# Attention block on one core: one 512 KB transposing DMA for both halves of a tile's probabilities

## Chip, cores and metric

One core of one Trainium2 chip. The metric is the device time of one execution in microseconds, the median of three runs. TensorE ran at its upper clock level, 2.4 GHz, through the whole profiled execution (granted clock 1.000).

## What is computed

The reference is an attention block with group normalisation in float32 on `x` of 4 x 128 x 32 x 32, so 4 batches of 128 channels and N = 1024 positions:

```python
h = x.reshape(B, GROUPS, C // GROUPS, N)            # 32 groups of 4 channels
h = (h - mean) * rsqrt(var + 1e-6)                  # over a group's channels and positions
h = h.reshape(B, C, N) * gamma[None, :, None] + beta[None, :, None]
qkv = einsum('oc,bcn->bon', w_qkv, h) + b_qkv       # q, k, v: 128 channels each
attn = softmax(einsum('bqc,bkc->bqk', q, k) / sqrt(C), axis=-1)
out = einsum('bqk,bkc->bqc', attn, v)
out = einsum('oc,bcn->bon', w_proj, out.transpose(0, 2, 1)) + b_proj
return x + out.reshape(B, C, H, W)
```

## The kernel before

The products that carry the accuracy are done in halves: a float32 value is split into a float16 high half and a float16 low half (the value less the high half), and three products (high by high, high by low, low by high) stand for one. The weights are folded ahead: `a_mat` joins the query and key weights, so that one product of `z` (the normalised input) gives `t`, and `t` by `z` gives the scores; `w_mat` joins the value and projection weights, so that `v` already holds the projected values.

The work is cut into G = 32 tiles of 128 query rows: 4 batches (b) of 8 tiles (s). A tile `g` goes through these steps, each on its own engine, held together by semaphores that count:

1. `score_tile(g)` on TensorE (lines 617 to 619): six matmuls of 512 columns give the 128 x 1024 scores in one of two PSUM slots. It waits until the exponential of tile g-2 has read the slot, and for `t_lo` of its batch half.
2. `maxima(g)` on VectorE (L432, L435): the row maximum and the bias of the exponential.
3. `exponentials(g)` on ScalarE (L343) writes `probs`, a ring of RING = 4 tiles; `p_high(g)` on ScalarE (L350) rounds it to the high half, `p_hl[:, g % RING, 0]`. It waits until the transposition of the high half of tile g-4 has landed.
4. `p_low(g)` on GpSimd (L285) writes the low half, `p_hl[:, g % RING, 1]`. It waits for the high half, and for the landing of tile g-4's low half.
5. SP transposes each half, 128 x 1024 float16 or 256 KB, by a DMA into `ptT`, a ring of PT_RING = 6 tiles (L232 the high half when it is made, L235 the low half when it is made).
6. `values(g)` on TensorE (lines 632, 633, 637): 16 matmuls of the high half against `v_hi` and `v_lo`, then, behind the wait for the low half's landing, 8 of the low half against `v_hi`, all 128 x 128 x 128 into one PSUM area.
7. `scale_output(g)` (L447), a turn on TensorE (L643) and `add_input(g)` (L453) finish the tile; SP stores four tiles at a time (L225).

The order of work is written out by hand, and each engine runs its own program in order. TensorE's loop takes, in step g: `score_tile(g)`, the turn of tile g-5, `values(g - 4)` (LAG = 4), and in some steps the products for `v` and for the next batch's `t`. So a tile's transpositions have about four steps of TensorE to land, and value matmuls that wait hold back the next score tile behind them. SP's program in step g: a wait that TensorE is done with tile g-6 (a free place in `ptT`), the wait for the high half and its DMA, the wait for the low half and its DMA, and, in every fourth step from 8 on, a store of tiles g-8 to g-5. GpSimd also normalises the next batch between its low halves: for batch 1 in steps 1, 3 and 4, for the later ones spread over the steps (lines 291 to 311).

Of the kernel before, what the change touches and what calls it, by code (L numbers as in the profile page):

```python
# [12 lines left out]
P = 128  # L13
B = 4
N = 1024
# [3 lines left out]
TILES = N // P  # L19
# [3 lines left out]
RING = 4  # L23
PT_RING = 6
# [12 lines left out]
def attention_block(nc, x, gamma, beta, w_qkv, b_qkv, w_proj, b_proj, out):  # L37
# [4 lines left out]
    with ExitStack() as ctx:  # L42
        def sb(name, shape, dt=F32):
            return ctx.enter_context(nc.sbuf_tensor(name, shape, dt))
# [4 lines left out]
        def sem(name):  # L49
            return ctx.enter_context(nc.semaphore(name))  # L50
# [56 lines left out]
        v_hi = sb("v_hi", [P, B * N], F16)  # L107
# [7 lines left out]
        p_hl = sb("p_hl", [P, RING, 2, N], F16)  # L115
        ptT = sb("ptT", [P, PT_RING, 2, TILES, P], F16)
# [71 lines left out]
        exp_ready = sem("exp_ready")  # L188
        phi_ready = sem("phi_ready")
        plo_ready = sem("plo_ready")  # L190
        hi_transposed = [sem(f"hi_transposed{i}") for i in range(RING)]
        lo_transposed = [sem(f"lo_transposed{i}") for i in range(RING)]
        pv_ready = sem("pv_ready")
        rinv_ready = sem("rinv_ready")
        oT_ready = sem("oT_ready")
# [8 lines left out]
        def wait(eng, s, value):  # L204
            if value > 0:
                eng.wait_ge(s, value)
# [3 lines left out]
        @block.sync  # L210
        def _(sp):
            for half in range(2):
                cols = slice(half * HALF, (half + 1) * HALF)
                sp.dma_start(x_sb[:, cols], x_d[0, :, cols]).then_inc(x_first[half], 16)
            sp.dma_start(beta_c[:], col(beta)).then_inc(c_loaded, 16)
            sp.dma_start(bq_c[:], col(b_qkv[0:P])).then_inc(c_loaded, 16)
            sp.wait_ge(wqk_loaded, 16)
            sp.wait_ge(gcol_loaded, 16)
            for b in range(1, B):
                sp.dma_start(x_sb[:, b * N:(b + 1) * N], x_d[b]).then_inc(x_rest[b - 1], 16)  # L220

            def store(first, tiles):
                b, s = divmod(first, TILES)
                sp.wait_ge(out_ready, first + tiles)
                sp.dma_start(out_d[b, :, s * P:(s + tiles) * P],  # L225
                             out_sb[:, first * P:(first + tiles) * P]).then_inc(stored, 16)

            for g in range(G):

                wait(sp, pv_ready, g - PT_RING + 1)  # L230
                sp.wait_ge(phi_ready, g + 1)
                sp.dma_start(ptT[:, g % PT_RING, 0], p_hl[:, g % RING, 0], transpose=True  # L232
                             ).then_inc(hi_transposed[g % RING], 16)
                sp.wait_ge(plo_ready, g + 1)
                sp.dma_start(ptT[:, g % PT_RING, 1], p_hl[:, g % RING, 1], transpose=True  # L235
                             ).then_inc(lo_transposed[g % RING], 16)
                done = g - LAG - CT
                if done >= 0 and done % CT == 0:
                    store(done, CT)
            for first in range(G - 2 * CT, G - CT, CT):  # L240
                store(first, CT)
            store(G - CT, CT - 1)
            store(G - 1, 1)
            sp.wait_ge(stored, 16 * (G // CT + 1))

        @block.gpsimd
        def _(pool):
            nc.gpsimd.memset(zero32[:], 0.0).then_inc(zeroed, 1)
            pool.wait_ge(zeroed, 1)
            nc.gpsimd.affine_select(out=ident32[:], in_=zero32[:], compare_op=ALU.not_equal, fill=1.0, base=0,  # L250
                                    pattern=[[-1, P]], channel_multiplier=1).then_inc(consts, 1)
            pool.dma_start(bv_c[:], col(b_qkv[2 * P:3 * P])).then_inc(o_loaded, 16)
            pool.dma_start(bp_c[:], col(b_proj)).then_inc(o_loaded, 16)

            def power(b):
                pool.wait_ge(vareps_ready, b + 1)
                nc.gpsimd.tensor_tensor(rstd[:, b:b + 1], var_eps[:, b:b + 1], minus_half[:], ALU.pow  # L257
                                        ).then_inc(rstd_ready, 1)

            def normalise(b, half):  # L260
                pool.wait_ge(rstd_ready, b + 1)

                pool.wait_ge(zlo_ready, b * 2)
                cols = slice(half * HALF, (half + 1) * HALF)
                nc.gpsimd.tensor_scalar(z32[:, cols], x_sb[:, b * N + half * HALF:b * N + (half + 1) * HALF],
                                        neg_mean[:, b:b + 1], rstd[:, b:b + 1], ALU.add, ALU.mult
                                        ).then_inc(z_ready, 1)

            def z_high(b, half):
                cols = slice(half * HALF, (half + 1) * HALF)  # L270
                pool.wait_ge(z_ready, b * 2 + half + 1)
                nc.gpsimd.tensor_copy(z_hi[:, b * N + half * HALF:b * N + (half + 1) * HALF], z32[:, cols]
                                      ).then_inc(zhi_ready, 1)

            def z_low(b, half):
                to = slice(b * N + half * HALF, b * N + (half + 1) * HALF)
                pool.wait_ge(zhi_ready, b * 2 + half + 1)
                nc.gpsimd.tensor_tensor(z_lo[:, to], z32[:, half * HALF:(half + 1) * HALF], z_hi[:, to],
                                        ALU.subtract).then_inc(zlo_ready, 1)

            def p_low(g):
                pool.wait_ge(phi_ready, g + 1)

                wait(pool, lo_transposed[g % RING], 16 * (g // RING))
                nc.gpsimd.tensor_tensor(p_hl[:, g % RING, 1], probs[:, g % RING], p_hl[:, g % RING, 0],  # L285
                                        ALU.subtract).then_inc(plo_ready, 1)

            pool.wait_ge(const_dve, 2)
            power(0)

            for g in range(G):
                b, s = divmod(g, TILES)
                p_low(g)
                if g == 1:
                    power(1)
                    normalise(1, 0)
                    normalise(1, 1)
                if g in (3, 4):
                    z_low(1, g - 3)

                if s == 7 and b + 2 < B:
                    power(b + 2)
                    normalise(b + 2, 0)

                if b >= 1 and b + 1 < B:
                    if s == 0:
                        normalise(b + 1, 1)
                    if s in (1, 3):
                        z_high(b + 1, s // 2)
                    if s in (2, 4):  # L310
                        z_low(b + 1, s // 2 - 1)

        @block.scalar
        def _(act):
# [31 lines left out]
            def p_high(g):  # L346
                act.wait_ge(exp_ready, g + 1)

                wait(act, hi_transposed[g % RING], 16 * (g // RING))
                nc.scalar.activation(p_hl[:, g % RING, 0], probs[:, g % RING], ACT.Copy).then_inc(phi_ready, 1)  # L350

            act.wait_ge(grow_psum, 1)
# [12 lines left out]
            for g in range(G):  # L365
                b, s = divmod(g, TILES)
# [212 lines left out]
        def _(pe):  # L579
# [41 lines left out]

            def values(g):
                b = g // TILES
                pe.wait_ge(hi_transposed[g % RING], 16 * (g // RING + 1))

                wait(pe, out_ready, g - 1)
                pe.wait_ge(vlo_ready, b * 2 + 2)
                dst = o_ps[:, g % 2, 0:P]
                for k in range(TILES):
                    keys = slice(b * N + k * P, b * N + (k + 1) * P)  # L630
                    hi = ptT[:, g % PT_RING, 0, k]
                    nc.tensor.matmul(dst, hi, v_hi[:, keys], start=(k == 0), stop=False)  # L632
                    nc.tensor.matmul(dst, hi, v_lo[:, keys], start=False, stop=False)  # L633
                pe.wait_ge(lo_transposed[g % RING], 16 * (g // RING + 1))
                for k in range(TILES):
                    keys = slice(b * N + k * P, b * N + (k + 1) * P)
                    last = nc.tensor.matmul(dst, ptT[:, g % PT_RING, 1, k], v_hi[:, keys], start=False,  # L637
                                            stop=(k == TILES - 1))
                last.then_inc(pv_ready, 1)

            def turn(g):
# [41 lines left out]
            for g in range(G + LAG + 1):  # L683
                b, s = divmod(g, TILES)
# [6 lines left out]
                if LAG <= g < G + LAG:  # L691
                    if g == LAG:
                        pe.wait_ge(vareps_ready, 2)
                    values(g - LAG)
# [53 lines left out]
```

## Time and profile before

| what | value |
|---|---|
| time before, median of 3 runs | 132.26 us (130.9 to 132.26) |
| the profiled execution: its own time | 131.82 us |
| its span, first to last instruction | 129.8 us |
| TensorE matmul busy | 114.6 us (88%) |
| VectorE, ScalarE, GpSimd busy | 93.9, 87.9, 85.4 us |
| DMA: SP's and ACT's transfers, share of 16 engines' span | 89.9% |
| transposing DMAs | 64 of 256 KB |

The span is what the engines' instructions take from the first to the last; the profiled execution took 2.0 us more than that around it. Busy shares are averages over the whole span, and a matmul's duration in the profile includes its pipeline, so that those of successive matmuls overlap. The chain of waits follows the work that ended last back to what released it; SPq stands for SP's own queue, in which an issued DMA takes time too. Times in the rows below are microseconds from the start of the span unless marked ns.

### The profile page before, as it was taken

How to read it: one execution, taken by the hardware profiler on the slowest of the kernel's cores; microseconds unless marked ns; L12 is line 12 of the kernel's file. 1: busy time of each engine (PE TensorE's matmuls, PEld its weight loads, DVE VectorE, ACT ScalarE, POOL GpSimd, SP SyncE). 2: the span in 40 equal slices, each digit the busy share in tenths (PEclk: the TensorE clock that was granted, in tenths of full speed). 3: DMA queues.
4: the chain of work that ended last, by engine and by line, in shares of the span. 5: the costliest groups of instructions: out<-in, count | busy, mean ns of one | idle time of the engine just before them, and what ended most of it. 6: DMA issues, size and time to landing. Idle time of an engine off the chain costs nothing.

```text
span 129.8 us, 3100 instructions
## 1 busy us (share of the span) xinstructions
PE 114.6 (88%) x1161; PEld 80.6 (62%) x1161; DVE 93.9 (72%) x242; ACT 87.9 (68%) x121; POOL 85.4 (66%) x60
## 2 busy tenths in 40 slices
PE   0599887988998999999989999999899999987671
PEld 0373544556775677667646776776467767767550
DVE  3659799999856967998569579776695797774222
ACT  1304429999778787877986878879868788785000
POOL 6010004879999897999759888998657666788200
PEclk9999999999999999999999999999999999999999
DMA  3692000797999999999999999999999999999990
GB/s 94 170 346 119 0 3 17 146 123 147 192 153 187 184 197 129 240 191 192 149 224 194 187 192 200 179 146 234 190 169 132 243 192 114 197 232 155 179 246 20
DMA packets 70670, 21.43 MB, mean 165 GB/s; under 512 B 68352, under 2 KB 69120, under 8 KB 70656
## 3 DMA queue, kind: packets, MB, share of 16 engines
q1 hardware_dynamic: 69888, 20.98, 89.9%
q10 hardware_dynamic: 704, 0.26, 0.8%
q8 instruction: 9, 0.15, 0.5%
q14 instruction: 5, 0.04, 0.1%
q0 software_dynamic: 64, 0.00, 0.0%
HBM read 2.36 MB, written 2.10 MB: 34 GB/s over the span
## 4 chain that ended last, share of the span: by engine, by line
PE 49%; DVE 23%; DMA 9%; ACT 7%; SPq 6%; issue 2%; ACTq 0%
DVE row_max L432 10%; PE scores L617 7%; DMA ptT<-p_hl 6%; PE o_ps L637 6%; PE scores L619 6%; PE scores L618 6%; PE o_ps L633 5%; PE o_ps L632 5%; SPq L232 4%; DVE t_lo L421 4%; DMA wqkv_sb<-in_L_conv_w_qkv_dram 3%; PE o_ps L643 3%; ACT probs L343 3%; DVE out_sb L453 3%; ACT p_hl L350 2%
## 5 line engine op out<-in xcount | busy, mean ns | idle before, releaser
L285 POOL TENSOR_TENSOR p_hl<-probs,p_hl 128x1024 f16<-128x1024 f32 x32 | 68.1, 2130 | 27.0 <-ACT p_hl L350 26.7
L432 DVE TENSOR_REDUCE row_max<-scores 128x1 f32<-128x1024 f32 x32 | 39.1, 1222 | 19.3 <-PE scores L619 19.1
L343 ACT ACTIVATE probs<-scores,exp_bias,esc 128x1024 f32<-128x1024 f32 x32 | 38.5, 1202 | 19.2 <-DVE exp_bias L435 19.2
L350 ACT ACTIVATE p_hl<-probs 128x1024 f16<-128x1024 f32 x32 | 33.8, 1057 | 1.0
L632 PE MATMUL o_ps<-v_hi,ptT 128*128 128x128 f16 x256 | 32.0, 219 | 0.4 <-DVE v_lo L427 0.4
L633 PE MATMUL o_ps<-v_lo,ptT 128*128 128x128 f16 x256 | 32.0, 219 | 0.0
L617 PE MATMUL scores<-z_hi,t_hi 128*128 128x512 f16 x64 | 24.3, 379 | 2.8 <-DVE t_lo L421 1.7
L632 PEld LDWEIGHTS o_ps<-v_hi,ptT 128*128 128x128 f16 x256 | 25.0, 98 | 2.3 <-issue 0.8
L633 PEld LDWEIGHTS o_ps<-v_lo,ptT 128*128 128x128 f16 x256 | 25.0, 98 | 0.2
L619 PE MATMUL scores<-z_hi,t_lo 128*128 128x512 f16 x64 | 24.3, 379 | 0.0
L618 PE MATMUL scores<-z_lo,t_hi 128*128 128x512 f16 x64 | 24.3, 379 | 0.0
L637 PE MATMUL o_ps<-v_hi,ptT 128*128 128x128 f16 x256 | 19.5, 219 | 1.0 <-DMA ptT<-p_hl 1.0
L447 DVE TENSOR_SCALAR oT_sb<-o_ps,rinv,w_max 128x128 f32<-128x128 f32 x32 | 12.8, 399 | 5.2 <-PE o_ps L637 5.2
L637 PEld LDWEIGHTS o_ps<-v_hi,ptT 128*128 128x128 f16 x256 | 15.6, 98 | 1.3 <-DMA ptT<-p_hl 1.3
L643 PE MATMUL o_ps<-ident,oT_sb 128*128 128x128 f32 x32 | 9.4, 295 | 3.7 <-DVE oT_sb L447 3.1
L453 DVE SCALAR_TENSOR_TENSOR out_sb<-o_ps,bo,x_sb 128x128 f32<-128x128 f32 x32 | 11.0, 343 | 2.1 <-PE o_ps L643 2.1
L617 PEld LDWEIGHTS scores<-z_hi,t_hi 128*128 128x128 f16 x64 | 6.4, 100 | 9.0 <-DVE t_lo L421 4.5
L643 PEld LDWEIGHTS o_ps<-ident,oT_sb 128*128 128x128 f32 x32 | 4.5, 140 | 10.7 <-DVE oT_sb L447 8.5
L619 PEld LDWEIGHTS scores<-z_hi,t_lo 128*128 128x128 f16 x64 | 6.2, 98 | 7.6
L618 PEld LDWEIGHTS scores<-z_lo,t_hi 128*128 128x128 f16 x64 | 6.2, 98 | 4.5
L435 DVE TENSOR_SCALAR exp_bias<-row_max,neg_esc 128x1 f32<-128x1 f32 x32 | 6.9, 214 | 1.1
L257 POOL TENSOR_TENSOR rstd<-var_eps,minus_half 128x1 f32<-128x1 f32 x4 | 2.2, 553 | 7.3 <-DVE var_eps L415 7.3
(109 smaller groups left out, 134.0 us busy)
## 6 DMA issues: line engine op xcount, KB each, us to landing
out_dram<-out_sb SPq DMA_DIRECT2D x7, 256.0 KB, 2.6
x_sb<-in_x_dram SPq DMA_DIRECT2D x3, 512.0 KB, 4.8
ptT<-p_hl SPq DMA_TRANSPOSE x64, 3.4
x_sb<-in_x_dram SPq DMA_DIRECT2D x2, 256.0 KB, 3.3
out_dram<-out_sb SPq DMA_DIRECT2D x1, 192.0 KB, 2.0
wqkv_sb<-in_L_conv_w_qkv_dram ACTq DMA_DIRECT2D x1, 128.0 KB, 4.0
wqkv_sb<-in_L_conv_w_qkv_dram ACTq DMA_DIRECT2D x1, 64.0 KB, 3.5
wp_sb<-in_L_conv_w_proj_dram ACTq DMA_DIRECT2D x1, 64.0 KB, 3.8
```

Source lines behind the costliest of these rows:

```text
L285: nc.gpsimd.tensor_tensor(p_hl[:, g % RING, 1], probs[:, g % RING], p_hl[:, g % RING, 0], ALU.subtract).then_inc(plo_ready, 1)
L343: nc.scalar.activation(probs[:, g % RING], scores[:, g % SLOTS], ACT.Exp, bias=exp_bias[:, g:g + 1], scale=esc[:], accum_out=row_sum[:, g: ...
L350: nc.scalar.activation(p_hl[:, g % RING, 0], probs[:, g % RING], ACT.Copy).then_inc(phi_ready, 1)
L432: nc.vector.tensor_reduce(row_max[:, g:g + 1], scores[:, g % SLOTS], AX_X, ALU.max).then_inc(max_ready, 1)
L453: nc.vector.scalar_tensor_tensor(out=out_sb[:, cols], in0=o_ps[:, g % 2, P:2 * P], scalar=bo[:], in1=x_sb[:, cols], op0=ALU.add, op1=ALU.a ...
L617: nc.tensor.matmul(dst, t_hi[:, rows], z_hi[:, cols], start=True, stop=False)
L618: nc.tensor.matmul(dst, t_hi[:, rows], z_lo[:, cols], start=False, stop=False)
L619: last = nc.tensor.matmul(dst, t_lo[:, rows], z_hi[:, cols], start=False, stop=True)
L632: nc.tensor.matmul(dst, hi, v_hi[:, keys], start=(k == 0), stop=False)
L633: nc.tensor.matmul(dst, hi, v_lo[:, keys], start=False, stop=False)
L637: last = nc.tensor.matmul(dst, ptT[:, g % PT_RING, 1, k], v_hi[:, keys], start=False, stop=(k == TILES - 1))
L643: nc.tensor.transpose(o_ps[:, g % 2, P:2 * P], oT_sb[:, g % 2], ident32[:]).then_inc(turned, 1)
```

## The change

Both halves of a tile go in one DMA, 128 x 2048 float16 or 512 KB, into the same places of `ptT`. SP issues it when the low half is made (`plo_ready`), and no longer waits for the high half alone. The two rings of landing semaphores become one, `transposed`. `p_high(g)` waits for the landing of all of tile g-4, and `p_low(g)` waits only for its high half. `values(g)` waits once, for the whole tile, and its 24 matmuls run in the order high, high, low for each block of 128 keys.

```diff
@@ -188,8 +188,7 @@
         exp_ready = sem("exp_ready")
         phi_ready = sem("phi_ready")
         plo_ready = sem("plo_ready")
-        hi_transposed = [sem(f"hi_transposed{i}") for i in range(RING)]
-        lo_transposed = [sem(f"lo_transposed{i}") for i in range(RING)]
+        transposed = [sem(f"transposed{i}") for i in range(RING)]
         pv_ready = sem("pv_ready")
         rinv_ready = sem("rinv_ready")
         oT_ready = sem("oT_ready")
@@ -228,12 +227,10 @@
             for g in range(G):
 
                 wait(sp, pv_ready, g - PT_RING + 1)
-                sp.wait_ge(phi_ready, g + 1)
-                sp.dma_start(ptT[:, g % PT_RING, 0], p_hl[:, g % RING, 0], transpose=True
-                             ).then_inc(hi_transposed[g % RING], 16)
                 sp.wait_ge(plo_ready, g + 1)
-                sp.dma_start(ptT[:, g % PT_RING, 1], p_hl[:, g % RING, 1], transpose=True
-                             ).then_inc(lo_transposed[g % RING], 16)
+                sp.dma_start(ptT[:, g % PT_RING].rearrange("p a k q -> p (a k) q"),
+                             p_hl[:, g % RING].rearrange("p a n -> p (a n)"), transpose=True
+                             ).then_inc(transposed[g % RING], 16)
                 done = g - LAG - CT
                 if done >= 0 and done % CT == 0:
                     store(done, CT)
@@ -279,9 +276,8 @@
                                         ALU.subtract).then_inc(zlo_ready, 1)
 
             def p_low(g):
+
                 pool.wait_ge(phi_ready, g + 1)
-
-                wait(pool, lo_transposed[g % RING], 16 * (g // RING))
                 nc.gpsimd.tensor_tensor(p_hl[:, g % RING, 1], probs[:, g % RING], p_hl[:, g % RING, 0],
                                         ALU.subtract).then_inc(plo_ready, 1)
 
@@ -346,7 +342,7 @@
             def p_high(g):
                 act.wait_ge(exp_ready, g + 1)
 
-                wait(act, hi_transposed[g % RING], 16 * (g // RING))
+                wait(act, transposed[g % RING], 16 * (g // RING))
                 nc.scalar.activation(p_hl[:, g % RING, 0], probs[:, g % RING], ACT.Copy).then_inc(phi_ready, 1)
 
             act.wait_ge(grow_psum, 1)
@@ -621,21 +617,17 @@
 
             def values(g):
                 b = g // TILES
-                pe.wait_ge(hi_transposed[g % RING], 16 * (g // RING + 1))
+                pe.wait_ge(transposed[g % RING], 16 * (g // RING + 1))
 
                 wait(pe, out_ready, g - 1)
                 pe.wait_ge(vlo_ready, b * 2 + 2)
                 dst = o_ps[:, g % 2, 0:P]
                 for k in range(TILES):
                     keys = slice(b * N + k * P, b * N + (k + 1) * P)
-                    hi = ptT[:, g % PT_RING, 0, k]
+                    hi, lo = ptT[:, g % PT_RING, 0, k], ptT[:, g % PT_RING, 1, k]
                     nc.tensor.matmul(dst, hi, v_hi[:, keys], start=(k == 0), stop=False)
                     nc.tensor.matmul(dst, hi, v_lo[:, keys], start=False, stop=False)
-                pe.wait_ge(lo_transposed[g % RING], 16 * (g // RING + 1))
-                for k in range(TILES):
-                    keys = slice(b * N + k * P, b * N + (k + 1) * P)
-                    last = nc.tensor.matmul(dst, ptT[:, g % PT_RING, 1, k], v_hi[:, keys], start=False,
-                                            stop=(k == TILES - 1))
+                    last = nc.tensor.matmul(dst, lo, v_hi[:, keys], start=False, stop=(k == TILES - 1))
                 last.then_inc(pv_ready, 1)
 
             def turn(g):
```

## Rows read from the trace of the kernel before

**Rows 1.** The page: busy time of TensorE, and DMA share in 40 slices

```profile
PE 114.6 (88%) x1161; PEld 80.6 (62%) x1161; DVE 93.9 (72%) x242; ACT 87.9 (68%) x121; POOL 85.4 (66%) x60
...
DMA  3692000797999999999999999999999999999990
```

**Rows 2.** The page: the chain that ended last, by engine

```profile
PE 49%; DVE 23%; DMA 9%; ACT 7%; SPq 6%; issue 2%; ACTq 0%
```

**Rows 3.** The chain in order of time, 25 to 45 us: start, us, what

```profile
34.80 0.45 PE o_ps L637 x8
...
39.93 0.39 PE scores L617
```

**Rows 4.** The chain in order of time, from 100 us

```profile
108.08 1.83 SPq L232
...
122.54 3.40 DMA ptT<-p_hl
...
125.98 0.64 PE o_ps L637 x8
```

**Rows 5.** Timeline of SP: start, us, queue, line, operation

```profile
26.03 2.40 SPq L235 DMA_TRANSPOSE ptT<-p_hl  x1
...
30.88 1.23 SPq L235 DMA_TRANSPOSE ptT<-p_hl  x1
...
53.95 1.27 SPq L232 DMA_TRANSPOSE ptT<-p_hl  x1
...
56.70 1.29 SPq L232 DMA_TRANSPOSE ptT<-p_hl  x1
...
106.35 1.23 SPq L235 DMA_TRANSPOSE ptT<-p_hl  x1
...
107.68 2.24 SPq L232 DMA_TRANSPOSE ptT<-p_hl  x1
...
114.10 0.58 SPq L225 DMA_DIRECT2D out_dram<-out_sb  x1
...
114.77 1.27 SPq L232 DMA_TRANSPOSE ptT<-p_hl  x1
...
118.99 2.12 SPq L235 DMA_TRANSPOSE ptT<-p_hl  x1
...
121.21 1.28 SPq L232 DMA_TRANSPOSE ptT<-p_hl  x1
```

**Rows 6.** Instructions on the tile ptT: durations in ns, and landing times

```profile
L232 SPq DMA_TRANSPOSE ptT<-p_hl x32: 1267/1287/2237, 21.2 to 121.2; - x32
...
DMA to landing us min/median/max: 3.1/3.4/5.0
```

**Rows 7.** Two stretches: busy time of engines, clock, DMA share, GB/s

```profile
22.40:23.80 1.40, 1.40 (x8) 0.73 (x9) 1.36 (x5) 1.40 (x3) 1.26 (x2) 1.00 1.00 187
...
62.70:63.70 1.00, 1.00 (x7) 0.45 (x6) 0.00 (x0) 0.97 (x3) 0.69 (x1) 1.00 0.85 16
```

**Rows 8.** Timeline of PE: first value matmuls of tiles 2, 26 and 31

```profile
33.74 0.22 PE L632 MATMUL o_ps<-v_hi,ptT 128*128 128x128 f16 x1
...
34.64 0.55 PE L637 MATMUL o_ps<-v_hi,ptT 128*128 128x128 f16 x7
...
112.06 0.22 PE L632 MATMUL o_ps<-v_hi,ptT 128*128 128x128 f16 x1
...
124.60 0.23 PE L632 MATMUL o_ps<-v_hi,ptT 128*128 128x128 f16 x1
```

**Rows 9.** What ACT waited for longest, and ACT's high half of tile 5

```profile
ACT probs L343 <- DVE exp_bias L435: 19.2, 27, 3.3
...
33.50 1.06 ACT L350 ACTIVATE p_hl<-probs 128x1024 f16<-128x1024 f32 x1
```

**Rows 10.** Timeline of POOL

```profile
28.74 4.21 POOL L285 TENSOR_TENSOR p_hl<-probs,p_hl 128x1024 f16<-128x1024 f32 x2
...
118.86 2.12 POOL L285 TENSOR_TENSOR p_hl<-probs,p_hl 128x1024 f16<-128x1024 f32 x1 [0.61 <-ACT p_hl L350]
```

## Prediction

> **What bounds the kernel now.** I read the page first. TensorE is busy 88% of the span, and the DMA digits stand at 9 in nearly every slice from the first transposition on [rows 1]. No engine's own work makes up the whole span, so the second view is the chain: half of it is PE, a quarter DVE, 9% DMA and 6% SP's queue [rows 2]. Read in order of time it has two regimes. From about 12 to 108 us it runs through PE in program order: the low products of tile 2 (34.80) lead to score tile 7, its maximum and the scores at 39.93 [rows 3]. Whatever delays PE there delays the next score tile, and with it everything up to the end. From 108.08 on it is SP and the DMA: the transpositions follow one another without a break until the low half of tile 31 lands at 125.94, and eight matmuls follow [rows 4]. The reader should carry away two questions: when does a tile's transposition land against the moment PE wants it, early on, and how long does SP's row of transpositions take at the end.
>
> **How a transposition costs now.** Back to back, SP goes from one tile's high half to the next one's in 2.75 us (53.95 to 56.70) [rows 5]; one 256 KB DMA lands 3.1 us at the least and 3.4 at the median after its issue starts [rows 6]. Alone in the queue (the first, issued at 21.2) it moves its bytes from 22.4 on and then holds the DMA engines at 1.00 for 1.40 us at 187 GB/s [rows 6, 7]. So two halves take the engines 2 x 1.38 = 2.76 us, which is SP's pace: SP is held by the transfer. A pair issued together lands 121.21 to 122.54 + 3.40 = 125.94, 4.73 us after its start [rows 4, 5].
>
> **The change, part by part.**
> - One DMA in place of two. The bytes are the same. It removes one issue, one wait and a gap of 0.05 us. The trace has no 512 KB transposition. Lower bound: it costs what a 256 KB one does, 3.4 us to land and 1.3 on SP. Upper bound: nothing moves before the whole issue is over; then it lands 2.62 (issue) + 2.06 (3.40 - 1.34, landing after the end of an issue) + 1.38 (second half) = 6.1 us after its start. Nearest row is the pair, 4.73 less the gap: I take L = 4.7 us to land and c = 2.7 us from one tile to the next on a busy SP.
> - It is issued when the low half is made, not when the high half is. The low half is POOL's 2.13 us behind. The early issue of the high half is what is lost.
> - PE's 24 value matmuls stand behind one wait. Before, 16 of them (0.90 us, from 33.74 to 34.64 in tile 2 [rows 8]) ran while the low half was still moving. Where the transposition is late, these 0.90 us come behind it. Reordering the 24 costs nothing: same operands, same loads.
> - The wait of ACT's high half moves to the combined landing. ACT shows no idle time for a transposition, only for DVE [rows 9], and tile 5's high half starts at 33.50 while tile 1, issued at about 26.03, lands by 26.03 + 4.7 + 1.07 = 31.8 (1.07 being the excess of the issue that stood there, 2.40 over 1.33) [rows 5]. Nothing, and 1.7 us of cover. Behind it on ACT would stand the next exponential.
> - POOL drops its own wait; ACT's covers it. It never waited for a DMA, so nothing.
> - SP's stores stand behind the combined issue. They had to wait for SP before too; cost nothing until the last one, which the tail sum contains.
>
> *First tiles.* POOL makes the low halves of tiles 2 and 3 in one stretch from 28.74 to 32.95, behind the normalising of batch 1, which no value product feeds; tile 2's is ready at 30.87 and SP issues at 30.88 [rows 5, 10]. Combined it lands 30.88 + 4.7 = 35.58. PE began tile 2's values at 33.74 [rows 8], because its high half had gone at 28.47. PE is late by 1.84 us, in the chain's first regime. Tiles 0 and 1 are late by less than 1 us by the same sum, and this swallows them, as tile 2's time is fixed by POOL. **+1.84.**
>
> *Middle.* All later work moves along by that amount, so I compare old times. The tightest tile that still has a score tile behind it is 26: low half issued 106.35, plus 4.7, plus 0.95 for a disturbance (the issue at 107.68 took 2.24 instead of 1.29) = 112.0; PE wants it at 112.06 [rows 5, 8]. The same sum leaves the others that have one 0.1 to 3 us. **+0**, but with no cover left: an L of 5.2 costs 0.5 here. These disturbances are stretches in which the DMA engines are 0.85 busy and move 16 GB/s [rows 7]; I keep them where they are.
>
> *Tail.* Starts on SP: tile 26 at 106.35; tile 27 at 106.35 + 2.7 + 0.95 = 110.0; tile 28 at 112.7; store 0.67 (114.10 to 114.77); tile 29 at 116.07; tile 30 at 118.77; tile 31 at 121.47 + 0.79 (2.12 - 1.33 at 118.99) = 122.26 [rows 5]. POOL has tile 31's low half at 118.86 + 2.12 = 120.98 [rows 10], so SP, not POOL, sets it. Landing 126.96, 0.05 to start, 0.90 for 16 matmuls and 0.64 for the last eight: 128.55. Before, 125.98 + 0.64 = 126.62 [rows 4]; PE had begun the high products at 124.60 [rows 8]. **+1.93**, of which 0.90 is the lost overlap and 1.02 the later landing.
>
> Sum: 1.84 + 1.93 = 3.77. The profiled execution took 131.82 us (span 129.8 and 2.0 around it), so 135.6 us. The runs have 130.9 to 132.26 with the median at 132.26, 0.3% above the profiled one; I state 135.6 and keep that 0.4 in the range. A measurement of this kernel can tell about 1%, 1.3 us, from no change.
>
> **Rivals.**
> - *The second half moves faster inside one DMA.* The rows show 187 GB/s for one 256 KB transposition [rows 7], which is the basis of my 1.38. If a large one ran at twice that, L = 3.4 + 0.7 = 4.1 and c = 2.0: tile 2 lands at 34.98, +1.24; at the tail SP has no backlog, tile 31 starts with POOL at 121.0, lands at 125.1, ends 125.1 + 1.59 = 126.7, +0.1. In all +1.3: 133.1. Against it: the DMA digits are 9 with issues back to back, so the engines and not the single issues set the pace.
> The Trainium skill would have it so (Advanced Engine Details and Errata, X-Bar Transpose (TRN2)): transposing DMAs run as fast as others, at an expected 350-400 GB/s; an estimate by that page for the second 256 KB is 0.7 us. The trace's 187 GB/s disagrees for halves; no run yet shows a 512 KB one.
> - *The bytes move only after the whole issue.* L = 6.1: first tiles +3.2, middle +1.2 to 1.4 as nothing covers it, tail +3.3: about 139.5. For it: the lone transposition started moving 1.24 us after its issue started, just when an issue of 1.29 ends [rows 6, 7]. Against: with a second issue blocked behind a first one, SP is held until the first has moved, so the queue between them holds little more than 256 KB and a larger one must move while it is issued (the issue after a disturbed one takes 2.24, rows 5).
> - *Not slower: cost is per DMA and not per byte.* Then L = 3.4 and SP is held 1.3 us. Tile 2 lands 34.28, +0.54; tile 31 at 121.0 + 3.4 + 1.59 = 126.0, -0.6; total 131.8. It decides where L is under 3.5. Against: the same DMA digits, and 1.40 us at a full share for half the bytes.
> - *The change is not what it says*: the build cuts the 512 KB in two again. Then both wait for the low half, L = 4.73 and c = 2.76: tail +0.3 more, 136.0, hardly to be told from the forecast except by 64 issues in the profile.
>
> **Chances.** Forecast 0.65; faster second half 0.15; late start of the bytes 0.08; cost per DMA 0.07; split again 0.05. The forecast and the last are slower; the late start is slower; the faster second half lies at +1.0%, half on each side; cost per DMA is mostly no change, 0.03 faster. Slower by over 1% 0.85, within 1% 0.12, faster 0.03. Range 132.9 to 138.2, inside the 131.8 and 139.5 that the two bounds of L make: below, the faster second half; above, an L of 5.3 (about +0.6 in each of three places on top) with the 0.4 of the median. It leaves out the per-DMA case and the full late start, 0.15.
>
> **What would show it.** 32 issues at one line, 2.5 to 2.7 us each, landing 4.6 to 4.8 after their start at the median. An idle time of PE before the values of tile 2, of about 1 to 1.8 us, ended by the DMA, near 35.6. All middle score tiles late by 1.8. No idle time of ACT for a transposition. At the end PE waits for tiles 29, 30 and 31, and all 24 matmuls of tile 31 follow its landing. The forecast falls if landings lie under 4.1 or over 5.3 us, if PE does not wait at tile 2, or if the 1.8 us are made good before tile 26.

## The result, and the profile after

The changed kernel took 136.74 us in the median of four executions (134.95 to 137.74) against 131.83 us for the kernel before in the same rounds: a ratio of 1.0305, 95% interval 1.0237 to 1.0372, so some 4 us slower. The medians and ranges here and below are of all executions of a kernel; the ratios, and the losses in us that go with them, leave out those more than 1.5% above the fastest. The profiled execution took 134.95 us, with a span of 133.3 us and a granted clock of 1.000: it is the fastest of the four, and 3.1 us above the profiled one of before. The other three had a mean clock of 0.972 to 0.987. So there are two things to explain: 3.1 us of schedule, and what the clock has to do with the rest.

The page of the changed kernel, its lines for TensorE, the DMA digits, the chain by engine, SP's transpositions and the wait for them (as in [rows 1] and [rows 2]; the two last lines are from the page's lists of costliest groups and of DMA issues):

```profile
PE 115.1 (86%) x1161; PEld 80.7 (61%) x1161; DVE 94.0 (71%) x242; ACT 88.2 (66%) x121; POOL 85.4 (64%) x60
...
DMA  3691000794999999999998799899989999999851
...
PE 55%; DVE 21%; DMA 10%; POOL 5%; ACT 4%; issue 3%; ACTq 0%; POOLq 0%; SPq 0%
...
L628 PE MATMUL o_ps<-v_hi,ptT 128*128 128x128 f16 x256 | 44.6, 219 | 4.7 <-DMA ptT<-p_hl 4.7
...
ptT<-p_hl SPq DMA_TRANSPOSE x32, 4.6
```

SP's queue, 6% of the chain before [rows 2], is at nothing, and POOL, which was not in it, is at 5%: what used to start on the high half now waits for the low half. TensorE sits idle for 4.7 us ahead of value matmuls until a transposition lands. Asked for the tile `ptT`, the trace gives SP's durations in ns and the landings, which answer to [rows 6]:

```profile
L231 SPq DMA_TRANSPOSE ptT<-p_hl x32: 1317/2092/3741, 23.4 to 122.8; - x32
...
DMA to landing us min/median/max: 4.3/4.6/5.6
```

There are 32 issues. A 512 KB transposition lands 4.6 us after its start at the median, where a pair took 4.73 and one half 3.4. SP is held for 1.3 to 3.7 us by one.

The chain in order of time from 20 to 45 us, the place of [rows 3]:

```profile
23.48 2.13 POOL p_hl L281
...
28.77 2.11 POOL p_hl L281
30.89 4.43 DMA ptT<-p_hl
35.37 0.23 PE o_ps L628
...
41.56 0.39 PE scores L613
```

Tile 2's low half is made at 30.88, its DMA is issued at 30.89 and lands at 35.32, and the values begin at 35.37 where they began at 33.74 [rows 8]: 1.63 us late. The scores at 39.93 [rows 3] are now at 41.56, again 1.63. The starts of the exponentials carry the same number without change from tile 7 to tile 31 (1.63 to 1.64 us in every tile). The end of the chain, the place of [rows 4]:

```profile
120.67 5.38 DMA ptT<-p_hl
126.09 0.23 PE o_ps L628
...
127.65 0.42 DVE oT_sb L443
128.11 0.33 PE o_ps L635
...
129.82 0.42 DVE oT_sb L443
...
130.65 0.35 DVE out_sb L449
```

The last value matmul ends 3.18 us later than before, so the end adds 1.55 to the 1.63.

### The profile page after: what moved, and what is told of

It reads as the page before. It is cut to its first block, busy times and chain, and to the rows that moved or that the text cites. A ratio compares the mean times of both kernels' runs of the same rounds, so it can differ in the third digit from the quotient of the medians.

```text
span 133.3 us, 3040 instructions
## 1 busy us (share of the span) xinstructions
PE 115.1 (86%) x1161; PEld 80.7 (61%) x1161; DVE 94.0 (71%) x242; ACT 88.2 (66%) x121; POOL 85.4 (64%) x60
## 4 chain that ended last, share of the span: by engine, by line
PE 55%; DVE 21%; DMA 10%; POOL 5%; ACT 4%; issue 3%; ACTq 0%; POOLq 0%; SPq 0%
DVE row_max L428 10%; DMA ptT<-p_hl 7%; PE scores L613 7%; PE o_ps L628 7%; PE scores L615 7%; PE scores L614 6%; PE o_ps L630 6%; PE o_ps L629 6%; POOL p_hl L281 3%; PE o_ps L635 3%; DVE t_lo L417 3%; DMA wqkv_sb<-in_L_conv_w_qkv_dram 3%; DVE out_sb L449 3%; DVE oT_sb L443 2%; PE scores L663 2%
## 5 line engine op out<-in xcount | busy, mean ns | idle before, releaser
L628 PE MATMUL o_ps<-v_hi,ptT 128*128 128x128 f16 x256 | 44.6, 219 | 4.7 <-DMA ptT<-p_hl 4.7
L629 PE MATMUL o_ps<-v_lo,ptT 128*128 128x128 f16 x256 | 44.5, 219 | 0.0
L630 PE MATMUL o_ps<-v_hi,ptT 128*128 128x128 f16 x256 | 44.5, 219 | 0.0
L628 PEld LDWEIGHTS o_ps<-v_hi,ptT 128*128 128x128 f16 x256 | 25.0, 98 | 7.4 <-DMA ptT<-p_hl 4.7
L630 PEld LDWEIGHTS o_ps<-v_hi,ptT 128*128 128x128 f16 x256 | 25.0, 98 | 0.0
L326 ACT ACTIVATE t_hi<-misc,ct 128x512 f16<-128x512 f32 x8 | 5.4, 677 | 2.8 <-PE misc L591 2.8
```

The lines of the kernel that those rows point to most:

```text
L630: last = nc.tensor.matmul(dst, lo, v_hi[:, keys], start=False, stop=(k == TILES - 1))
```

## The experiments

Each is told as an edit of the kernel before or of the changed one. `ONE` is the set of tiles that go in one DMA with the changed kernel's waits and matmul order, the others are as before. "Step" is by how much the exponentials start later than in the profile of before, both counted from tile 0's; the tail is the additional delay of the last value matmul. All measured ratios are against the kernel before in the same rounds.

**late_pair.** Both halves still in a DMA each, but late.

```diff
-                sp.wait_ge(phi_ready, g + 1)
+                sp.wait_ge(plo_ready, g + 1)
                 sp.dma_start(ptT[:, g % PT_RING, 0], ...)
-                sp.wait_ge(plo_ready, g + 1)
                 sp.dma_start(ptT[:, g % PT_RING, 1], ...)
```

(and `values` with one wait for both landings, high, high, low.)

> Two DMAs of 256 KB as before, but both issued only when the low half is made, and all 24 value matmuls behind both landings. Theory (the loss is the later issue of the high half and the later start of the values, not the size of the DMA): as the changed kernel, span 133.3 us or up to 0.4 more, about +3.5 us on before, tile 2's values at 35.3 to 35.5. Rival (one large DMA is itself the slower one): close to before, at most +1 us.

Measured: 138.59 us, ratio 1.0518 (1.0446 to 1.0591). The rival is out: with two DMAs of the old size, issued late, the kernel is as slow as with one of 512 KB, and rather slower: +6.8 us, where I gave it +3.5. Its profile is no clean copy of the changed kernel's, though. Two stretches of it, with the columns of [rows 7] (PEclk is the third figure from the end):

```profile
26.00:30.00 4.00, 1.67 (x22) 1.13 (x20) 3.57 (x9) 3.97 (x7) 3.80 (x4) 1.00 1.24 157
30.00:33.40 3.40, 3.40 (x17) 1.77 (x15) 0.41 (x1) 1.76 (x4) 3.40 (x3) 0.50 0.67 126
```

TensorE was busy for 1.67 of the 4 us before 30.0, waiting for tile 0, and then had its clock at 0.50 (1.2 GHz, the lower level) for 3.4 us. The step was 3.22 us at tile 5 already, 3.10 at tile 7. Tile 2, with TensorE that late, was no longer waited for: it had landed at 34.98 and its values began at 36.35. The time of tile 2's values had another cause here than the one I expected. Unlike the changed kernel's, the step then grew, to 3.96 at tile 31, and the tail was 2.71, with a second fall of the clock at 125.6.

**one_wait.** DMAs as before, one wait ahead of all 24 matmuls.

```diff
                 pe.wait_ge(hi_transposed[g % RING], 16 * (g // RING + 1))
+                pe.wait_ge(lo_transposed[g % RING], 16 * (g // RING + 1))
```

> DMAs issued as before; only TensorE changes: one wait for both halves ahead of the 24 value matmuls, in the order high, high, low. Theory: tile 2's low half lands at 34.04 where the values began at 33.74, so +0.3 us there; at the end tile 31's low half lands at 125.9 and 1.54 us of matmuls follow where 0.64 did, +0.9 us; together +1.2 us on before. Rival (the order of the matmuls or the single wait costs in every tile): 0.05 us or more in each of 32 tiles, so over +2.5 us.

Measured: 134.22 us, ratio 1.0207 (1.0175 to 1.0239), 2.7 us, over twice what I gave it. The profile has a step of 0.47 us at tile 7, 0.77 at tile 31, and a tail of 1.44. The total is as high as the rival's, but its mechanism is not there: its price per tile is 0.05 us or more, and the step grows by 0.30 over 24 tiles, 0.013 each, so the order and the single wait cost next to nothing in the middle. I had both parts too small: the step was 0.77 in the end and not 0.3, and the tail 1.44 and not 0.9, since tile 31's low half landed 0.5 us later than the step explains, and 0.97 us more of matmuls stand behind it than before. So with both halves sent as early as before, the single wait alone delays the last value matmul by 2.21 us, where the whole change delays it by 3.18.

**split_first.** `ONE = range(4, 32)`.

> The changed kernel with tiles 0 to 3 as before (two DMAs, low products behind their own wait). Theory: PE begins tile 2's values at 33.7 again and the middle runs as before, so the changed kernel's time less 1.6 us, +1.7 us on before, all of it after 108 us; and if the long idle time of PE near tile 2 is what lowers its granted clock in some executions, the clock stays at 1.00 in all. Rival (the loss accrues over the tiles, each in one large DMA): no more than 4/32 of the loss goes, about +3.1 us on before.

Measured: 134.13 us, ratio 1.0195 (1.0130 to 1.0261), +2.6 us. The exponentials of all 32 tiles start within 0.01 us of before: the step is gone, and 28 tiles in one DMA put nothing in its place. The one execution with a clock of 1.00 took 133.07 us, 1.5 us above the 131.55 of before, close to the +1.7 expected; the other three (134.0 to 134.7, clock 0.986 or 0.987) are where the second half of the expectation failed. In the profile the clock fell too, at the other end, and the tail was 2.50:

```profile
40.00:120.00 80.00, 76.44 (x860) 55.97 (x857) 60.09 (x143) 63.06 (x84) 64.30 (x40) 1.00 1.06 187
124.80:128.20 3.40, 2.89 (x27) 2.56 (x25) 0.76 (x2) 0.00 (x0) 0.00 (x0) 0.50 0.37 131
```

**split_last.** `ONE = range(0, 28)`.

> The changed kernel with tiles 28 to 31 as before. Theory: the first tiles keep their +1.6 us; at the end the high products of tile 31 run again before its low half lands, but SP's row of transpositions still starts with tile 27 at its low half, so +0.3 to +0.6 of the tail's 1.6 us remains: +2.0 us on before. Rival (loss accrues evenly): +3.1 us.

Measured: 135.64 us, ratio 1.0311 (1.0266 to 1.0356), +4.1 us, twice the forecast. The step was 3.35 us instead of 1.63, with TensorE's clock down from 30.0 to 33.4 as in late_pair; the tail was 0.73, against 1.55 in the changed kernel and the 0.3 to 0.6 expected. So the tail's share came out near the expectation and the first tiles' did not. The clock is not all of it: the one execution with a clock of 1.000 took 134.80 us, 3.25 us above before, and no trace shows what it lost that on.

**warm_pe.** The changed kernel, and ahead of tile 0's values:

```diff
                     if g == LAG:
                         pe.wait_ge(vareps_ready, 2)
+                        for _ in range(KEEP_WARM):
+                            nc.tensor.matmul(o_ps[:, 1, 0:HALF], ones16[:], warm[:], start=True, stop=True)
```

> The changed kernel, and TensorE fills its wait for tile 0's landing with four matmuls of 512 columns whose result is not used. Theory (part of the loss in some executions is TensorE's granted clock falling for a stretch that begins in this wait, near 30 us): no fall near 30 us in any execution, the steps of the schedule stay as in the changed kernel's profile (tile 2 late by 1.6 us, span 133.3), so a median of 134.9 to 135.5 with less spread than 134.95 to 137.74. Rival (the fall has nothing to do with the wait): a spread up to 137.7 as before and a clock of 0.97 in some executions.

Measured: 136.52 us (134.41 to 136.96), ratio 1.0310 (1.0238 to 1.0383). It is no faster. The profile shows what it did and what it did not do. The chain, and two stretches:

```profile
22.92 6.31 DMA ptT<-p_hl
29.27 0.23 PE o_ps L651
```

```profile
27.40:28.20 0.80, 0.17 (x1) 0.00 (x0) 0.80 (x2) 0.78 (x1) 0.80 (x2) 1.00 2.13 20
...
30.00:33.40 3.40, 3.40 (x47) 2.73 (x43) 1.66 (x3) 1.80 (x4) 3.40 (x3) 1.00 0.72 139
...
122.30:129.10 6.80, 5.16 (x46) 4.84 (x47) 0.76 (x2) 0.00 (x0) 0.00 (x0) 0.50 0.77 174
```

Tile 0's 512 KB landed 6.31 us after its issue, not 4.57 as in the changed kernel's own profile. For nearly a microsecond in between 20 GB/s move, against 214 from 24.25 to 26.00 in the same profile. (The share of 2.13 counts each packet's whole duration in the stretch in which it starts; packets that start here take up to 1.6 us.) That is the disturbance of [rows 7]; in each profile it coincides with one of the nine packets of 16 KB that the page lists as queue q8, kind "instruction". Before, it fell at 26.8 on tile 1's halves, when tile 0's two had landed. A tile 0 in one DMA is still in flight at that time. In the changed kernel's own profile the packet came at 23.4, before any of tile 0's bytes moved. The four matmuls kept the clock at 1.00 from 30.0 to 33.4, and the step is 1.67 us, not the 3.1 to 3.6 of late_pair, split_last and pool_order, where tile 0 was as late and the clock fell. But the clock fell at 122.3, for 6.8 us, and the tail was 3.86. The clock is not alone in that: the disturbance also met tile 29, which landed 6.39 us after its issue, and its values began at 123.43, some 2.8 us later than before and the step together explain.

**split_ends.** `ONE = range(4, 26)`.

> Tiles 0 to 3 and 26 to 31 in two DMAs as before, tiles 4 to 25 in one of 512 KB. Theory: tiles in the middle land before TensorE wants them, so a combined one costs nothing there and the time is that of before within 0.5 us. Rival (loss by tile): 22/32 of +4 us, +2.7 us.

Measured: 132.99 us, ratio 1.0116 (1.0077 to 1.0155), +1.5 us: neither. The exponentials of tiles 26 to 31 start within 0.01 us of before, so TensorE lost nothing in the middle. SP did. Its timeline (start, us, line; compare the times 106.35, 107.68 and 121.21 of [rows 5], this profile's times are 0.5 us smaller for the same work):

```profile
102.44 2.91 SPq L239 DMA_TRANSPOSE ptT<-p_hl  x1
105.44 1.26 SPq L247 DMA_TRANSPOSE ptT<-p_hl  x1
106.75 2.31 SPq L251 DMA_TRANSPOSE ptT<-p_hl  x1
109.15 1.27 SPq L247 DMA_TRANSPOSE ptT<-p_hl  x1
...
121.75 1.27 SPq L247 DMA_TRANSPOSE ptT<-p_hl  x1
```

Tile 25 in one DMA (102.44) holds SP until 105.35, so tile 26's high half leaves at 105.44 where it left at 104.1 on this profile's scale, and tile 27's at 109.15 where it left at 107.2. The row of transpositions that sets the end is entered 2 us late. It makes 1 us of that good by tile 31, and the clock fell at 121.9 as well; the tail is 1.73.

**pool_order.** The changed kernel, GpSimd's normalising of batch 1 moved behind tile 2's low half.

```diff
-                if g == 1:
+                if g == 2:
                     power(1)
                     normalise(1, 0)
                     normalise(1, 1)
```

> The changed kernel, with GpSimd making tile 2's low half ahead of the normalising of batch 1 (which moves behind it). Theory (tile 2 is late because its low half stands behind the normalising): tile 2's low half is ready near 28.3 and lands at 33 to 33.5, so TensorE does not wait 1.4 us for it and most of the 1.6 us goes; but batch 1's normalised input comes 1 to 2 us later and ScalarE waits for it before tile 4's and 5's exponentials, which gives back up to 1 us: +0.5 to +1.6 us less than the changed kernel. Rival (the landing of tile 2 is late for a reason of the DMA, such as its queue behind tiles 0 and 1): tile 2 lands at 35.3 as now and nothing is gained.

Measured: 136.61 us (134.85 to 137.92), ratio 1.0315 (1.0258 to 1.0371). Nothing is gained. The mechanism itself is there: tile 2's low half was made at 27.82 and its DMA, issued at 28.76, landed at 33.13 instead of 35.32 (1.6 us earlier, as this profile's times are 0.6 us smaller for the same work), so the rival is wrong about the landing; ScalarE waited 0.87 us for the normalised input. But in this profile tile 0 landed 6.3 us after its issue, the clock fell from 29.9 to 33.3, and the step was 3.33, in which tile 2 has no part. In the one execution with a clock of 1.00 it took 134.85 us, no less than the 134.95 of the changed kernel. The tail was 2.52, with a second fall at 125.5. The run does not show what moving tile 2 alone is worth.

**store_later.** The kernel before, with the store of tiles 20 to 23 behind the last transposition.

```diff
-                if done >= 0 and done % CT == 0:
+                if 0 <= done < G - 3 * CT and done % CT == 0:
                     store(done, CT)
-            for first in range(G - 2 * CT, G - CT, CT):
+            for first in range(G - 3 * CT, G - CT, CT):
```

> The kernel before, with the store of tiles 20 to 23 moved from between the transpositions of tiles 28 and 29 to behind those of tile 31. Theory (from tile 27 on SP's row of transpositions sets the end): the 0.67 us of the store's issue and the 0.7 us of its transfer leave that row, tile 31 lands 0.7 us earlier, -0.5 to -0.7 us on before. Rival (the end is set by the low half on GpSimd): 0.

Measured: 131.11 us against 131.23, ratio 0.9987 (0.9963 to 1.0012): nothing. The chain of its last part, in order of time:

```profile
112.93 2.14 POOL p_hl L301
...
115.09 5.22 DMA ptT<-p_hl
...
120.99 0.87 SPq L247
...
121.91 3.41 DMA ptT<-p_hl
```

With the store gone SP runs into POOL: it waits for tile 29's low half at 115.07. That wait is short: tile 29's low half leaves 0.55 us earlier than before, on this profile's scale. The disturbance then holds it for 5.2 us, and the last tile leaves only 0.2 us earlier than before. So most of the store's time was lost again behind the disturbance, a little of it to POOL; this is one profile, and the times say no more than that the whole is worth nothing.

**changed_again.** The changed kernel unaltered, in more executions.

> The changed kernel unaltered, in more executions, each with its granted clock. Theory (the schedule costs +3.2 us, and a fall of TensorE's clock adds to it in some executions): executions at a clock of 1.00 near 134.9 us, those at 0.985 near 136, those at 0.97 near 137.6, median between 135.5 and 137. Rival (the spread has other causes): no order between clock and time.

Measured: 137.61 us, ratio 1.0447 (1.0385 to 1.0509). One of the six ran at a mean granted clock of 0.857 (145.16 us), and it is the profiled one. Two stretches of it:

```profile
20.00:30.80 10.80, 8.49 (x56) 4.71 (x57) 9.84 (x26) 10.54 (x16) 7.76 (x6) 0.85 0.67 93
31.00:34.00 3.00, 3.00 (x16) 1.60 (x14) 0.41 (x1) 1.68 (x4) 3.00 (x3) 0.50 0.50 93
```

Its clock was 0.85 nearly throughout, for which nothing here gives a cause. But it is the second profile of the unaltered kernel, and not like the first: the 16 KB packet came at 27.9, tile 0 landed 6.28 us after its issue, the clock was at 0.50 for 3.4 us from 30.9 on, and the step was 3.62 at tile 5. It is left out of the table. The others, with the four of the first result, which did not run beside them:

```
clock   1.000   0.985-0.987              0.972-0.975                      0.958
us      134.95  135.91, 136.51, 136.58   137.19, 137.56, 137.74, 138.50   138.03
```

Clock and time go together, as the theory has it, except for the last one. A single fall is 3.4 us at half clock in the traces, which is 0.013 of the mean over 134 us: by that the groups are none, one, two and three falls, the first of them worth 1 to 1.6 us. It is not worth that in every kernel: one_wait took 134.22 and 134.25 us at 0.987 and 133.86 and 134.23 us at 1.000. In the same rounds the kernel before had clocks of 0.995 to 1.000 in 16 of 17 executions; the other had 0.951 and took 139.78 us. The two results for this kernel, 1.0305 and 1.0447, differ; among the later executions none had a clock of 1.000.

**warm_both.** warm_pe's matmuls, and five more ahead of the values of tiles 29, 30 and 31.

```diff
+                    if g >= G + 1:
+                        pe.wait_ge(exp_ready, G)
+                        for _ in range(KEEP_WARM + 1):
+                            nc.tensor.matmul(scores[:, 0, 0:HALF], ones16[:], warm[:], start=True, stop=True)
                     values(g - LAG)
```

> The changed kernel with four unused matmuls in TensorE's wait for tile 0 and five in each of its waits for tiles 29, 30 and 31. Theory: the clock is at 1.00 in all executions up to the last store, and the median is 134.3 to 135.2, 1 to 2 us under the changed kernel's. Rival (clock falls are not worth time, since TensorE waits anyhow): the same median as the changed kernel's or more, as the extra matmuls stand ahead of the values.

Measured: 137.07 us (136.58 to 137.26), ratio 1.0419 (1.0371 to 1.0467). The clock stayed at 0.996 to 1.000 in all four executions and the spread shrank to 0.7 us, but the time did not go down; as a remedy it failed. The chain says why:

```profile
116.93 6.46 DMA ptT<-p_hl
123.44 0.23 PE o_ps L651
...
125.79 1.08 PE scores L725 x5
...
129.04 1.08 PE scores L725 x5
```

Tile 29 was hit by the disturbance. After it TensorE had no wait left for tiles 30 and 31, whose transpositions had landed by then, and the five matmuls stood on the chain twice, 2.16 us. Without them these executions would lie at 134.4 to 135.1, which is arithmetic and was not run. What the clock is worth at the end can be read beside warm_pe's profile, in which tile 29 was hit alike and the clock was at 0.50. The 24 value matmuls of tile 29 took 2.74 us there and 1.51 here, those of tile 30 took 2.56 and 1.50. That is 2.3 us for a fall of 6.8 us. The rival is wrong about that, but right about the time.

**two_for_tile2.** `ONE` is all tiles but 2.

> The changed kernel, with tile 2 alone in two DMAs. Theory: the step of 1.63 us in the score tiles from tile 7 on comes from tile 2 alone; it goes down to what tile 0's later landing leaves, 0.3 to 0.6 us, in an execution without a fall of the clock near 30 us (with one, tile 0 sets a step of 3.2 to 3.6 from tile 5 on and tile 2 changes nothing). Rival (the first tiles' loss is spread over them): 1.2 us or more remains.

Measured: 135.85 us (134.10 to 137.93), ratio 1.0237 (1.0164 to 1.0310). Its profile is one with the fall (clock 0.50 from 29.3 on): step 3.46 at tile 5 and 3.24 from tile 6, as the bracket of the expectation says. The case without a fall left only times, 134.10 and 135.11 us at clocks of 0.997 and 1.000, around the 134.95 of the changed kernel. How small the step is with tile 2 alone mended is not shown.

**split_from_20.** `ONE = range(4, 20)`.

> Two DMAs for tiles 0 to 3 and 20 to 31, one of 512 KB for tiles 4 to 19. Theory (with two DMAs from tile 26 on, SP came into its last row 2 us late because tile 25 was still in one; a combined tile costs nothing where the row behind it has time to catch up): as before within 0.4 us. Rival (each combined tile costs a little): 16/22 of the +1.5 us that 22 of them cost, +1.1 us.

Measured: 132.13 us against 131.54, ratio 1.0058 (1.0029 to 1.0086): +0.8 us, between what I allowed and the rival's. The interval, +0.4 to +1.1 us, just reaches both. Against split_ends, the six tiles 20 to 25 back in two DMAs take half of its loss away, where the rival has the loss by tile and would take a quarter; that difference is not clear of the two intervals either. What speaks against the rival is the profile. No exponential from tile 10 on starts over 0.01 us late. In the profile the tail is 0.46, with the disturbance on tile 27's low half (an issue of 1.97 us at 109.83) instead of its high half.

No version beat the kernel before. Keeping tiles 20 to 31 and 0 to 3 in two DMAs loses least of those with any in one.

## Why the prediction was right, and where not

The measured 136.74 us lies in the range of 132.9 to 138.2, 1.1 us above the 135.6 forecast; the direction was forecast too. The mechanism held; the agreement to 1 us has some luck in it, since one term was too large and another was missing.

- *L = 4.7 us, "nearest row is the pair".* Median 4.6, from 4.3 to 5.6. The rivals' landings fall with it: not 3.4 (cost per DMA), not 4.1 (faster second half), not 6.1 (late start of the bytes), and with 32 issues the DMA was not split again. But of the faster second half one part came out: its c = 2.0, where the median hold of SP was 2.09. The Trainium skill's 350-400 GB/s (Advanced Engine Details and Errata, X-Bar Transpose (TRN2)) are not borne out: the second 256 KB inside the same DMA adds 1.2 us to the landing (4.6 against 3.4), 220 GB/s, and the measurement decides.
- *"2.5 to 2.7 us each" on SP.* Wrong: 1.3 to 3.7, with a median of 2.09, and 1.90 for tile 2's; c = 2.7 was the term of the sum that was too large. SP is let go long before the transfer ends. It cost nothing, as SP's next tile had to wait for POOL or for the engines anyway.
- *First tiles, +1.84.* The place and the cause as told; 1.63 measured, because tile 2 landed after 4.43 us and not 4.7.
- *"Tiles 0 and 1 are late by less than 1 us [...] and this swallows them".* True in the profiled execution: tile 0 was 0.5 us late at its values, and of that 0.02 were left in the exponential of tile 6. It fails in many of the others, and this is the step that missed something. I had put the disturbance near 26 us on tile 1, because there it stood; but tile 0, now in flight for longer, can meet it: it landed after 6.2 to 6.4 us in all six of the experiments' profiles that have it in one DMA, the one of the unaltered kernel in changed_again among them. The profile that came with the result, with 4.57, is the exception. Alone that makes a step of 1.7 us instead of 1.63 (warm_pe), since tile 2 is late anyway. Together with the clock it makes 3.2 to 3.6, so the fall near 30 us is worth some 1.7.
- *Middle, +0.* Right: one step of 1.63 and none after it (changed kernel), none at all with tiles 4 to 31 in one DMA (split_first).
- *Tail, +1.93.* 1.55 measured, of other parts. The landing of tile 31 was only 0.31 late beyond the step, not 1.02. The forecast had SP back to back from tile 26 on, at c = 2.7. In fact SP waited for POOL on tiles 26 and 27 and caught up between. The lost overlap gave 0.88 of the forecast 0.90. And 0.36 was not in the sum: tile 31 had landed at 127.87, but TensorE had tile 30's turn ahead of its values, behind VectorE's scaling, and began them at 128.28.
- *Sum, 3.77 against 3.13 in the profiled execution.* The clock, which the forecast does not speak of, makes up for the difference in the median: the executions with a lower clock took 1 to 3.6 us more, eight of nine.
- *Range, 132.9 to 138.2.* The terms given for its upper end make 135.6 + 3 x 0.6 + 0.4 = 137.8. The measured median lies under either.

What stays open: what the falls cost in the median, as the worth read above is from single pairs of profiles, and no run holds the clock at the end without adding to the chain; and whether the q8 packets are what holds the transpositions, or come with it. Taking them away was not tried.

## What to carry to other kernels

Joining two transfers of which one is ready earlier costs the earlier one's head start, and it is paid where a consumer has no cover: in the first tiles of a pipeline, before the lag has built up, and in the last ones, where the queue itself sets the end. Tally for each tile the landing against the moment it is wanted; the mean over the kernel hides both places. And a wait that a profile of one execution prices at half a microsecond can, in other executions, also meet a disturbance and cost the engine its clock: run a changed kernel several times and read the granted clock of each.

## What the runs showed of the hardware that I had not expected

- A 512 KB transposition holds SP for 1.3 to 3.7 us and lands after 4.3 to 5.6 (32 of them in one profile); two of 256 KB together hold it for 2.6 to 2.8. The issue does not last as long as the transfer.
- TensorE's granted clock fell to 0.50 (1.2 GHz) for 3.4 us or twice that in this single-core program: at 30.0 us after it had been busy for 1.67 of 4 us, and near 122 to 126 us among the waits of the last tiles. It did not fall at 30 us in warm_pe's profile, where TensorE had been busy for 2.30 of the same 4 us. The same kernel showed none, one or more falls from execution to execution, going by the mean clocks. One execution of it had a granted clock of 0.85 nearly throughout and took 145.16 us.
- A disturbance of about 1 us in the DMA engines, beside one 16 KB packet of the kind "instruction": there are nine such packets in each profile. They come at other times in other versions of the kernel, and in the unaltered changed kernel the first came at 23.4 us in one profile and at 27.9 in the other. Transpositions that meet it land 1 to 2 us late: 4.96 for 3.4 at 116 us before, 6.3 for 4.6 at tile 0 in warm_pe.
